# The nets' first layer moved between x's first two blocks, with a new order of the first loads

## The reference

```python
def _ln(x, g, b):
    m = jnp.mean(x, axis=-1, keepdims=True)
    v = jnp.mean((x - m) ** 2, axis=-1, keepdims=True)
    return (x - m) * jax.lax.rsqrt(v + EPS) * g + b

def _mlp_ln(s, W1, b1, W2, b2, g, b):
    h = jax.nn.silu(s @ W1 + b1) @ W2 + b2
    return _ln(h, g, b)

h = _ln(x, pw_g[pathway_ids], pw_b[pathway_ids])
h = _ln(h, cp_g[compartment_ids], cp_b[compartment_ids])
t = _ln(x, tm_g[time_steps], tm_b[time_steps])
m = x + _mlp_ln(memory_state, mem_W1, ...)[:, None, :]
n = x + _mlp_ln(noise_state, noi_W1, ...)[:, None, :]
r = x + _mlp_ln(resource_state, res_W1, ...)[:, None, :]
s = _ln(x, ms_g[scale_type], ms_b[scale_type])
w = jax.nn.softmax(aw)
cat = jnp.concatenate([w[0] * h, w[1] * t, w[2] * m, w[3] * n, w[4] * r, w[5] * s], axis=-1)
out = x + _mlp_ln(cat, int_W1, int_b1, int_W2, int_b2, int_g, int_be)
```

## Time and profile before

| | |
|---|---|
| median of 3 runs | 929.16 us (928.73 to 929.22) |
| profiled execution | 928.64 us, span 926.9 us |
| TensorE busy | 919.0 us, 99% of the span |
| VectorE busy | 825.6 us, 89% |
| ScalarE busy | 326.7 us, 35% |
| GpSimd busy | 472.5 us, 51% |
| mean granted TensorE clock | 0.998 of full speed |

### The profile page before, as it was taken

One profiled execution on the slowest core, in us unless ns is written; L12 is line 12 of the kernel. 1 busy time (PEld: TensorE's weight loads), 2 busy tenths in 40 slices (PEclk: granted clock), 3 DMA queues, 4 the chain that ended last, 5 costly groups with the idle time before them and its releaser, 6 DMA issues.

```text
span 926.9 us, 13511 instructions
## 1 busy us (share of the span) xinstructions
PE 919.0 (99%) x4194; PEld 747.9 (81%) x4194; DVE 825.6 (89%) x1204; ACT 326.7 (35%) x415; POOL 472.5 (51%) x578
## 2 busy tenths in 40 slices
PE   9999999999999999999999999999999999999997
PEld 8777888888888888888888888888888888888885
DVE  7889999899898989989899898989989898998955
ACT  5835234252332514234242333424233251423412
POOL 5556473545545464563645546464563645446141
PEclk9999999999999999999999999999999999999999
DMA  9984757738566583856738465683856748475451
GB/s 333 358 307 148 227 163 244 196 89 279 154 206 179 164 267 102 254 142 234 197 112 281 139 214 161 197 244 91 268 139 239 182 137 276 120 241 145 126 114 45
DMA packets 99619, 178.75 MB, mean 193 GB/s; under 512 B 10129, under 2 KB 49041, under 8 KB 95633
## 3 DMA queue, kind: packets, MB, share of 16 engines
q1 hardware_dynamic: 44512, 95.88, 29.1%
q0 software_dynamic: 22976, 66.07, 27.9%
q10 hardware_dynamic: 32112, 16.58, 6.1%
HBM read 145.75 MB, written 32.75 MB: 193 GB/s over the span
## 4 chain that ended last, share of the span: by engine, by line
PE 97%; DVE 1%; DMA 1%; POOL 1%; ACT 0%; issue 0%; POOLq 0%; DVEq 0%; SPq 0%
PE hid_ps L1620 25%; PE hid_ps L1621 25%; PE hid_ps L1622 25%; PE o_ps L1707 3%; PE o_ps L1706 3%; PE made_ps L1707 3%; PE made_ps L1706 3%; PE o_ps L1708 3%; PE made_ps L1708 3%; PE made_ps L1563 1%; DMA keep<-int_W 1%; PE hid_ps L1627 0%; PE o_ps L1532 0%; PE o_ps L1520 0%; PE o_ps L1521 0%; PE o_ps L1548 0%
## 5 line engine op out<-in xcount | busy, mean ns | idle before, releaser
L1620 PE MATMUL hid_ps<-cat_hi,w_hi 128*128 128x512 f32 x1008 | 394.5, 391 | 0.0
L1622 PE MATMUL hid_ps<-cat_hi,w_lo 128*128 128x512 f32 x1008 | 392.3, 389 | 0.0
L1621 PE MATMUL hid_ps<-cat_lo,w_hi 128*128 128x512 f32 x1008 | 392.3, 389 | 0.0
L1620 PEld LDWEIGHTS hid_ps<-cat_hi,w_hi 128*128 128x128 f32 x1008 | 189.2, 188 | 46.2 <-issue 7.4
L1622 PEld LDWEIGHTS hid_ps<-cat_hi,w_lo 128*128 128x128 f32 x1008 | 189.2, 188 | 39.6
L1621 PEld LDWEIGHTS hid_ps<-cat_lo,w_hi 128*128 128x128 f32 x1008 | 189.3, 188 | 38.5
L617 POOL DMA_INDIRECT pw_rows<-pw,path_now x64 | 73.6, 1149 | 123.4 <-DVE y_sb L1147 106.6
L638 POOL DMA_DIRECT2D r_sb<-x x60 | 57.5, 958 | 108.2 <-DVE r_sb L1225 105.5
L853 ACT ACTIVATE cat_hi<-v_ring 128x1024 fp32r<-128x1024 f32 x30 | 31.9, 1062 | 201.2 <-DMA v_ring<-h_turned 201.2
L624 POOL DMA_INDIRECT pw_rows<-cp,class_now x64 | 84.1, 1313 | 32.7 <-issue 13.0
L845 ACT ACTIVATE cat_hi<-v_ring 128x1024 fp32r<-128x1024 f32 x64 | 66.4, 1059 | 84.1 <-DVE v_ring L1091 37.9
(11 more groups left out here) (199 smaller groups left out, 1385.4 us busy)
## 6 DMA issues: line engine op xcount, KB each, us to landing
x_sb<-xp SPq DMA_DIRECT2D x16, 1024.0 KB
out<-r_sb SPq DMA_DIRECT2D x63, 256.0 KB, 2.0
xc<-xT SPq DMA_DIRECT2D x15, 1024.0 KB, 9.3
h_turned<-y_sb ACTq DMA_DIRECT2D x60, 256.0 KB
r_sb<-x POOLq DMA_DIRECT2D x60, 256.0 KB, 4.2
v_ring<-h_turned SPq DMA_DIRECT2D x60, 256.0 KB
stats_bc<-token_stats SPq DMA_DIRECT2D x15, 512.0 KB
ids_sb<-ids SPq DMA_DIRECT2D x16, 256.0 KB
```

Of the source, the lines that this page charges most:

```text
L1620: pe.matmul(acc, w1_hi[:, k, cols], hi, start=start, stop=False)
L1621: pe.matmul(acc, w1_hi[:, k, cols], lo, start=False, stop=False)
L1622: return pe.matmul(acc, w1_lo[:, k, cols], hi, start=False, stop=stop)
```

## The change

The nets' first layer moves on TensorE from behind part 3 to between part 0 and part 1, with 13 warm matmuls ahead of it in place of 15. It writes to `made_ps` in place of `o_ps`. Its tiles move up on SyncE's queue ahead of `keep_load(2)`, and ScalarE copies its result (`nets_rows`) ahead of `sum_first(2)`. x^T's first feature tile comes alone on ScalarE's queue, its second on SyncE's behind the first sum's blocks, and both are split one at a time. The table comes ahead of x^T's second half. Of the statistics of batch 0, VectorE makes the variance plus epsilon and the negated mean (`x_moments`), GpSimd the power and one product. `first_fill(0)` waits for `nets_rows` in addition, since it writes the same PSUM tile.

```diff
-WARM = (30, 15)
+WARM = (30, 13)
...
             keep_load(0)
+            sp.dma_start(xc[:, 1, :], xT[0][:, TOKENS:2 * TOKENS]).then_inc(first_xT_in[1], 16)
             load_x(0)
             keep_load(1)
+            sp.dma_start(tab_raw, tabs).then_inc(table_in, 16)
             load_xT_half()
-            sp.dma_start(tab_raw, tabs).then_inc(table_in, 16)
+            for n in NET:
+                if tiles[n][1] < P:
+
+                    sp.wait_ge(stage_cleared, 1)
+                stage_load(n)
             keep_load(2)
...
             load_kinds(0)
-            for n in NET:
-                if tiles[n][1] < P:
-
-                    sp.wait_ge(stage_cleared, 1)
-                stage_load(n)
...
             def x_rstd(b):
...
-                nth = 1 if isinstance(b, int) and b == 0 else b + 2
-                rstd(xaggr, TT * (b + 1), xve, xve_done, xrs, xrs_done, xmv, slice(0, TT), nth)
                 if isinstance(b, int) and b == 0:
-
+                    pool.wait_ge(xve_done, 2)
+                    pool.tensor_tensor(xrs[:, :], xve[:, :], minus_half[:, :], ALU.pow).then_inc(xrs_done, 1)
                     pool.wait_ge(xrs_done, 1)
-                    pool.tensor_tensor(xmr[:, :], xmv[:, :, 0], xrs[:, :], ALU.mult).then_inc(xve_done, 1)
-                    pool.wait_ge(xve_done, 2)
-                    pool.tensor_tensor(xnmr[:, :], c_zero, xmr[:, :], ALU.subtract).then_inc(xrs_done, 1)
+                    pool.tensor_tensor(xnmr[:, :], xmr[:, :], xrs[:, :], ALU.mult).then_inc(xrs_done, 1)
                     return
...
+            def x_first_high(k):
+                act.wait_ge(first_xT_in[k], 16)
+                act.activation(cat_hi[:, 0, k, :], xc[:, k, :], ACT.Copy).then_inc((first_x_hi, x_hi_done)[k], 1)
...
-                act.activation(net_h[:, :], o_ps[:, 0, :], ACT.Copy).then_inc(net_hid_rows, 1)
+                act.activation(net_h[:, :], made_ps[:, 0, :], ACT.Copy).then_inc(net_hid_rows, 1)
...
-            load_xT_half()
+            act.dma_start(xc[:, 0, :], xT[0][:, 0:TOKENS]).then_inc(first_xT_in[0], 16)
...
             sum_first(0)
-            x_high(0, 0)
+            x_first_high(0)
             sum_high(0)
+            x_first_high(1)
             sum_first(1)
-            x_high(0, 1)
             act.wait_ge(table_in, 16)
...
+            x_high(0, 1)
             sum_high(1)
+            nets_rows()
             sum_first(2)
...
                 w_high(5)
-                nets_rows()
                 w_high(6)
...
+            def x_first_low(k):
+                dve.wait_ge((first_x_hi, x_hi_done)[k], 1)
+                dve.tensor_tensor(cat_lo[:, 0, k, :], xc[:, k, :], cat_hi[:, 0, k, :].bitcast(f32),
+                                  ALU.subtract).then_inc((first_x_lo, x_lo_done)[k], 1)
+
+            def x_moments():
+                dve.wait_ge(xaggr, TT)
+                dve.wait_ge(half_ready, 6)
+                dve.tensor_tensor(xve[:, :], xmv[:, :, 1], eps_col[:, :], ALU.add).then_inc(xve_done, 1)
+                dve.tensor_scalar(xmr[:, :], xmv[:, :, 0], -1.0, None, ALU.mult).then_inc(xve_done, 1)
...
                 sum_blocks(0)
-                x_low(0, 0)
+                x_first_low(0)
                 sum_low(0)
+                x_first_low(1)
                 gain_signs()
                 for t in range(TT):
                     x_stats(0, t)
+                x_moments()
                 sum_blocks(1)
...
             def nets_hidden():
 
-                pe.wait_ge(xhat_copied, 2)
...
-                    pe.matmul(o_ps[at:at + 32, 0, :], sT[:, c, :], stage[NET[c] % STAGE], start=True, stop=True).then_inc(pe_used, 1)
+                    pe.matmul(made_ps[at:at + 32, 0, :], sT[:, c, :], stage[NET[c] % STAGE], start=True, stop=True).then_inc(pe_used, 1)
 
             def nets_hidden_turn():
-                pe.wait_ge(net_hid_rows, 1)
+                pe.wait_ge(xhat_copied, 2)
...
                     pe.wait_ge(tables_ready, 1)
+                    pe.wait_ge(net_hid_rows, 1)
...
                 warm(WARM[1])
+                nets_hidden()
                 x_high_part(1)
...
                 x_low_part(3)
-                nets_hidden()
                 first_fill(1)
```

More of the change, by code:

```diff
@@ L190, in build @@
         sum_in = [sem(f"sum_in{k}") for k in range(FT)]
-        sum_more_in = [sem(f"sum_more_in{k}") for k in range(FT)]
+        sum_more_in = [sem("sum_more_in")]
         stage_in = [sem(f"stage_in{i}") for i in range(STAGE)]
@@ L233, in build @@
         xT_in = sem("xT_in")
-        xT_half_in = sem("xT_half_in")
+        first_xT_in = [sem(f"first_xT_in{k}") for k in range(2)]
+        first_x_hi = sem("first_x_hi")
+        first_x_lo = sem("first_x_lo")
         ids_in = sem("ids_in")
@@ L550, in x_rstd @@
                 wait(pool, pack_turned, b - 1)
-                nth = 1 if isinstance(b, int) and b == 0 else b + 2
-                rstd(xaggr, TT * (b + 1), xve, xve_done, xrs, xrs_done, xmv, slice(0, TT), nth)
                 if isinstance(b, int) and b == 0:
+                    pool.wait_ge(xve_done, 2)
+                    pool.tensor_tensor(xrs[:, :], xve[:, :], minus_half[:, :], ALU.pow).then_inc(xrs_done, 1)
                     pool.wait_ge(xrs_done, 1)
-                    pool.tensor_tensor(xmr[:, :], xmv[:, :, 0], xrs[:, :], ALU.mult).then_inc(xve_done, 1)
-                    pool.wait_ge(xve_done, 2)
-                    pool.tensor_tensor(xnmr[:, :], c_zero, xmr[:, :], ALU.subtract).then_inc(xrs_done, 1)
+                    pool.tensor_tensor(xnmr[:, :], xmr[:, :], xrs[:, :], ALU.mult).then_inc(xrs_done, 1)
                     return
+                rstd(xaggr, TT * (b + 1), xve, xve_done, xrs, xrs_done, xmv, slice(0, TT), b + 2)
                 pool.nop(nofuse=True)
@@ L750, in _ @@
         def _(act):
-            def load_xT_half():
-                act.dma_start(xc[:, 0:2, :].rearrange("q f j -> q (f j)"), xT[0][:, 0:2 * TOKENS]).then_inc(xT_half_in, 16)
+            def x_first_high(k):
+                act.wait_ge(first_xT_in[k], 16)
+                act.activation(cat_hi[:, 0, k, :], xc[:, k, :], ACT.Copy).then_inc((first_x_hi, x_hi_done)[k], 1)
             def sum_first(k):
@@ L837, in x_high @@
             def x_high(b, i):
-                act.wait_ge(xT_half_in if isinstance(b, int) and b == 0 and i == 0 else xT_in, 16 * (b + 1))
+                act.wait_ge(xT_in, 16 * (b + 1))
                 wait(act, used, 6 * (b - 1) + 5 + i)
@@ L1662, in x_high_part @@
                 pe.wait_ge(sum_hi_done, k + 1)
-                pe.wait_ge(x_hi_done, k // 2 + 1)
+                pe.wait_ge(first_x_hi if k == 0 else x_hi_done, k // 2 + 1)
                 for h in range(FT):
                     pe.matmul(hid_ps[:, h, :], w1_hi[:, k, h * P:(h + 1) * P], hi, start=(k == 0), stop=False)
-                pe.wait_ge(x_lo_done, k // 2 + 1)
+                pe.wait_ge(first_x_lo if k == 0 else x_lo_done, k // 2 + 1)
                 for h in range(FT):
```

## The result

The changed kernel takes 930.86 us (median of 17 runs, 930.51 to 931.54) against 928.78 us of the kernel before in the same sessions (17 runs, 928.53 to 929.35). The ratio is 1.0022, interval 1.0016 to 1.0028: 2.1 us slower. That is clear of no change, but not of the 0.2% at which the forecast drew its line: the interval reaches from 0.16 to 0.28%. So the forecast "same" holds, though barely, and its range holds too, while its size was a third of what came (+0.71 us). Its 929.9 us also stood on the 929.16 of three runs; from the 928.78 of 17 runs the same sum gives 929.5. The profiled execution has a span of 929.1 us in 930.8 us, before 926.9 in 928.64.

A forecast was written before the change was run, and what follows sets the result against it. TensorE bounds the kernel, with no wait after 20.43 us. Moving that wait by +1.71 us, less 1.00 us for the nets' layer, gave +0.71 us on 929.16: 929.9 us, range 928.1 to 931.2.

The forecast's parts named there:

- "same": Whole kernel: time within about 0.2% (1.9 us) of the kernel before; chance 0.86.
- The nets' layer, -1.00 us: TensorE: the layer leaves its place behind the last wait, giving back 1.00 us, and costs nothing in its new place.
- The tiles of the nets at 15.9: SyncE's queue: the nets' tiles land at 15.9 us; over a microsecond later would still cost nothing.
- keep_load(2) at 19.25: SyncE's queue: landing moves from 16.1 by 1.9 us of bytes and 1.25 us of lag, TensorE's wait by +1.71.
- the lag of 1.25 us: DMA queues: one engine of 16 falls about 1.25 us behind at an instruction fetch, delaying every later load.
- ScalarE: nets_rows hides; sum_first(2) starts at 19.25, normalisations end at 22.09, TensorE goes on at 22.14 for 20.43.
- The statistics: VectorE and GpSimd: the chain is some 1 us shorter and starts earlier, but brings nothing.
- the first block: TensorE's part 0: can't start before the warm matmuls end at 10.10, so an earlier first block gains nothing.
- the later lag: keep_load(3) lands at 22.0, wanted at 22.5; row ids delay gathers by 1.9 us, within 2.16 us of cover.
- The first: Rival: the lag misses keep_load(2), which lands at 18.0; -0.54 us, 928.6 us; chance 0.25.
- second: Rival: keep_load(2) lands by 17.6 and TensorE's wait is not moved; -0.94 us, 928.2 us; chance 0.07.
- The third: Rival: TensorE's clock falls in the longer wait of 2.3 us, costing 1.94 us; +2.65 us, 931.8 us; chance 0.10.

The follow-up runs named there:

- e5: Kernel before, with only the statistics of batch 0 split between VectorE and GpSimd as in the changed kernel: 928.60 us.
- e10: e1 with 12 warm matmuls added between part 1 and the transposes: 931.06 us.
- e1: Kernel before, with only the nets' four tiles loaded ahead of keep_load(2) and nothing done earlier with them: 932.21 us.
- e6: Kernel before, with only x^T's first two tiles split over ScalarE's and SyncE's queues: 928.88 us.
- e11: e9 with the nets' last two tiles loaded as the same bytes over 128 partitions: 928.98 us.
- e9: e8 with the table's load moved behind keep_load(2) and its conversions behind the third sum's: 929.00 us.
- e12: e9 with ScalarE's order of the change put back (nets_rows, sum_first(2), then three normalisations): 929.38 us.
- e7: Changed kernel, with the nets' third and fourth tiles loaded as the same bytes over 128 partitions: 929.73 us.
- e3: Changed kernel, with x^T's first two tiles again as one load on ScalarE's queue: 930.04 us.
- e4: Changed kernel, with ScalarE normalising three tiles of x before nets_rows and sum_first(2): 930.24 us.
- e8: e3 with ScalarE's order x_norm(0), x_norm(1), sum_first(2), x_norm(2), nets_rows: 929.57 us.

## Why the prediction was right and wrong

*The nets' layer, -1.00 us.* Right: span less start of part 2 is 904.8 to 905.0 in every kernel with the layer moved, and 905.8 or 905.9 in the kernel before, e5 and e10 (e1 had the slow clock on top; e6, at 906.2, is 0.3 off, and the cause of that is open).

*The tiles of the nets at 15.9.* Wrong by 2.5 us: the last is there at 18.4. The aside that this "stays at nothing" if they are late held, but by luck: it held because the normalisations were late too. Part 1 ended at 22.3, behind the 22.09 at which the forecast had the normalisations done. Less its two waits, TensorE would have started part 2 at 24.24 - 0.73 = 23.5, while the forecast's sum puts that start at 21.06 + 1.71 = 22.8. So by this estimate the late tiles alone, with `keep_load(2)` on time, would have cost 0.7 us more than forecast.

*keep_load(2) at 19.25.* This is the term that was mis-sized; it landed at 20.7. The 1.9 us of bytes and the lag of 1.25 us were right: with neither narrow tiles nor the split, e11 lands where these two terms put it, and e9 and e12 put the lag at 1.4 us. The reason given for meeting the lag, that the fetch stays where it was, was wrong: it started at 16.9 in the changed kernel and not at 15.8. The load was met all the same, since it too came later. What failed is "the queues moved 381 GB/s in this stretch", taken for all bytes, whatever their tiles: the narrow tiles took 1.0 us more in the changed kernel (e7), and the split of x^T, which I had only as a small help to the first block, cost 0.9 us at this load (e3). These two overlap, since e3 alone also lifts the rate in the stretch of the narrow tiles, and together make the missing 1.45 us.

*ScalarE.* The chain behind the landing was right to 0.1 us: 20.71 + 0.63 + 2.21 = 23.55, and TensorE went on at 23.61. From the forecast's landing the same chain gave 22.14, so the error of 1.47 us stands in the landing; the late tiles were a second one, hidden behind it. The copy hid, as forecast, though it came 2.5 us late.

*The statistics, the first block, the later lag.* Nothing each, as forecast (e5, and TensorE has no wait behind the start of part 2). The first block did not come earlier but 0.2 us later (part 0 at 10.18 for 9.96), which the later waits hid. `keep_load(3)` came at 23.4 and was taken at 23.98; the row ids came 3.3 us late and still no wait of TensorE followed.

*The rivals.* The first and second did not come in the changed kernel; the escape from the lag that the first one needs is seen in e9. The third did not come either, but e1 shows it in the wait that it named, at 1.5 us in place of the 1.94 of its price.

*The chances.* 0.86 for "same" hung on a sum of +0.71, and 930.86 lies on the line between "same" and "slower". The range reached 931.2 for "a longer lag, a late gather"; neither came, and it held by luck, because two terms that it does not name (narrow tiles, the split) were of that size. I gave a later landing no case of its own among the chances, although any further 1.2 us there was "slower". A rate read in one stretch and used for other tiles deserved one.

## What to carry over

A load that is moved up a full queue is paid for by every load behind it; price it in bytes, and price tiles of 64 or 32 partitions apart, by a window in which such tiles went by (here 273 GB/s from 22 to 24 us, against 381), and not by the mean rate. The 1.0 us that TensorE gained stood against 1.9 us of bytes ahead of the load on which its last wait hung, and none of the three other orders of ScalarE that were run (e4, e8, e12) won that back. Where an expected landing lies within a microsecond of an instruction fetch, treat it as two cases, and prefer an order of the waiting engine that bears both.

## What the runs showed of the hardware

- Transfers into 64 and 32 partitions took 1.0 us more than the same 192 KB over 128 partitions, at a DMA share that stayed near 1.0 (252 against 392 GB/s from 15 to 18 us, e7); about 0.6 of it without the split of x^T (311 GB/s, e3).
- One instruction fetch of 0.02 MB came with a load that completed 1.4 us later, by one of its 16 shares (17.9 and 19.3 us for the same queue, e9 and e12). What decides when the fetch starts (between 15.8 and 17.5 us in these kernels) stays open.
- With one of two x^T tiles moved to the second queue, the same bytes in all, the later loads were complete 0.7 to 0.9 us later (`keep_load(1)` at 12.8 in e6 and 13.0 in the changed kernel, 12.1 without it).
- After a wait of 1.5 us and a transpose of 0.33, with two shorter waits behind it, TensorE was granted 0.51 of its clock from 22 to 24 us (e1; by their times in three runs of five). With 2.8 us of warm matmuls in the gap it stayed at 1.00 (e10, all ten runs by their times).
